# Gated attention kernel, one core: the first group's row step moved into the last feed-forward chunk, comparisons in two pieces, statistics on other half-steps

## The reference

```
xn = layernorm(x)                      # x: 8 batches x 1024 tokens x 512
q, k, v = xn @ Wq.T, xn @ Wk.T, xn @ Wv.T            # 16 heads of 32
attn = softmax(q @ k.T * 512 ** -0.5) + rel_bias     # the bias is added after the softmax
s = layernorm(attn @ v) * gamma + beta
h = square(relu(xn @ W_fc.T)); y = h @ W_proj.T      # W_fc: 2048 x 512
g = silu(spikes(y) / 5)                # spikes: how often a 5-step recurrence fires; 5 thresholds on y
out = x + s * g
```

## Time and profile before

| what | value |
|---|---|
| time, median of 3 runs (lowest to highest) | 3539.49 us (3537.76 to 3540.11) |
| the profiled execution: its time, its span | 3539.38 us, 3537.6 us |
| PE, ACT, DVE, POOL busy, share of the span | 97%, 74%, 71%, 49% |
| granted PE clock, mean | 0.996 of full speed (2.4 GHz) |
| feed-forward ends, attention begins | at about 1399 us of the span |

### The profile page before, as it was taken

How to read it: one execution, slowest core, us unless ns; L and a number is a source line. 1 busy time by engine, 2 the same in 40 slices (tenths; PEclk the granted TensorE clock), 3 DMA queues, 4 the chain that set the end, 5 groups by cost and what they waited for, 6 DMA issues and landing times.

```text
span 3537.6 us, 55268 instructions
## 1 busy us (share of the span) xinstructions
PE 3424.5 (97%) x19964; PEld 1440.8 (41%) x19964; DVE 2496.7 (71%) x3948; ACT 2628.4 (74%) x3926; POOL 1718.1 (49%) x997
## 2 busy tenths in 40 slices
PE   7999999999999999999999999999999999999996
PEld 3444444444444444433433433433433433433431
DVE  5555555555555545777888888888888788888887
ACT  6433333333333335999999999999999999999997
POOL 0012222111111123799675675675675675676662
PEclk9999999999999999999999999999999999999999
DMA  5122322332222222221422322322322322322322
GB/s 186 57 80 80 104 79 87 101 98 94 79 79 80 80 82 75 87 74 51 141 85 80 100 86 80 101 85 80 100 86 80 101 85 81 100 85 81 100 63 81
DMA packets 238751, 312.35 MB, mean 88 GB/s; under 512 B 96624, under 2 KB 132208, under 8 KB 238480
## 3 DMA queue, kind: packets, MB, share of 16 engines
q1 hardware_dynamic: 238480, 308.82, 28.1%
HBM read 174.65 MB, written 76.61 MB: 71 GB/s over the span
## 4 chain that ended last, share of the span: by engine, by line
ACT 37%; issue 10%; PE 8%; DVE 4%; SPq 1%; DMA 1%; ACTq 0%; DVEq 0%; POOL 0%; POOLq 0%
ACT recurrence_or_probs L1380 19%; ACT s_sb L1387 18%; DVE s_sb L1462 2%; PE misc L1249 2%; PE acc L1329 2%; PE s_ps L1309 2%; PE s_ps L1295 2%; DVE gate_or_tokens L1574 1%; DVE x_or_queries L1499 1%; SPq L253 0%; DMA xT<-xnT 0%; DVE outT L1482 0%; DVE gate_or_tokens L1577 0%; DMA x_or_queries<-sub_rows 0%; PE misc L1231 0%
## 5 line engine op out<-in xcount | busy, mean ns | idle before, releaser
L1462 DVE TENSOR_SCALAR_CACHE_REDUCE s_sb<-s_ps 128x1024 f32<-128x1024 f32 x998 | 1213.3, 1221 | 366.8 <-PE s_ps L1295 337.8
L1650 POOL TENSOR_TENSOR recurrence_or_probs<-recurrence_or_probs,toep 128x512 f32<-128x512 f32 (+1 forms) x375 | 1287.4, 3452 | 361.2 <-ACT recurrence_or_probs L1380 360.9
L1387 ACT ACTIVATE s_sb<-s_sb,nmax 128x1024 f32<-128x1024 f32 x998 | 1164.9, 1167 | 5.3 <-DVE s_sb L1462 5.3
L1380 ACT ACTIVATE recurrence_or_probs<-s_ps 128x1024 f32<-128x1024 f32 x1024 | 1059.3, 1036 | 6.5 <-PE s_ps L1309 6.4
L486 PE MATMUL ps_fc<-xnT_part,w_fc 128*128 128x512 f16 x3072 | 707.2, 380 | 4.5 <-DVE w_fc L734 4.5
L501 PE MATMUL ps_y<-w_pr,hid_part 128*128 128x512 f16 x3072 | 706.2, 380 | 3.5 <-issue 2.6
L127 POOL TENSOR_TENSOR recurrence_or_probs<-gate_or_tokens,beta_row 128x512 f32<-128x512 f32 x60 | 89.9, 1498 | 1110.0 <-DVE gate_or_tokens L182 1106.5
L658 ACT ACTIVATE relu<-ps_fc 128x512 f32<-128x512 f32 x256 | 152.8, 597 | 630.3 <-PE ps_fc L486 630.1
L842 DVE TENSOR_TENSOR hid<-relu 128x512 f32<-128x512 f32 x256 | 212.8, 831 | 510.4 <-ACT relu L658 510.4
L1329 PE MATMUL acc<-recurrence_or_probs,val 128*32 128x512 f32 x4096 | 545.1, 604 | 2.3 <-DVE recurrence_or_probs L1561 1.5
L486 PEld LDWEIGHTS ps_fc<-xnT_part,w_fc 128*128 128x128 f16 x3072 | 301.0, 98 | 368.9 <-issue 7.8
(11 more groups left out here) (172 smaller groups left out, 2673.1 us busy)
## 6 DMA issues: line engine op xcount, KB each, us to landing
toep<-table_rows SPq DMA_DIRECT2D x32, 2048.0 KB, 8.2
x_or_queries<-x_or_queries SPq DMA_DIRECT2D x384, 64.0 KB, 2.0
x_or_queries<-in_x SPq DMA_DIRECT2D x16, 1024.0 KB, 10.4
xnT<-xnT_part SPq DMA_DIRECT2D x32, 512.0 KB, 8.3
x_or_gate<-in_x SPq DMA_DIRECT2D x16, 1024.0 KB, 9.2
base<-x_or_gate SPq DMA_DIRECT2D x16, 1024.0 KB, 6.8
xT<-xnT SPq DMA_DIRECT2D x32, 512.0 KB, 9.6
result<-gate_or_tokens SPq DMA_DIRECT2D x64, 256.0 KB, 2.0
```

Source lines behind the costliest of these rows:

```text
L1380: nc.scalar.activation(prob[:, k % PROBS, 2 * second:2 * second + 2, :].rearrange("p j n -> p (j n)"), s_ps[:, item_buffer(pair_item(m)), ...
L1387: nc.scalar.activation(s_sb[:, i % 4, :], s_sb[:, i % 4, :], ACT.Exp, bias=nmax[:, par, j, st:st + 1], scale=-1.0, accum_out=den[:, par, j ...
L1462: nc.vector.tensor_scalar(s_sb[:, i % 4, :], s_ps[:, item_buffer(tile_item(n)), :], -1.0, None, ALU.mult, ALU.min, accum_out=nmax[:, par, ...
L1650: nc.gpsimd.tensor_tensor(tile, tile, toep[:, par, :, at:at + width], ALU.add).then_inc(biased, 1)
```

## The change

It has four parts, and the program computes the same values.

1. The row step of group 0 (logarithm, six POOL instructions, four matmuls, copy, four transfers) leaves the prelude and is placed in the last feed-forward chunk: the logarithm in step 10, the POOL instructions ahead of the gate's products, the matmuls in step 15 into `ps_t`, the copy in step 15, the transfers at the end of SP's chunk. The constants that it needs are written by POOL at the start of the program (`set_constants`) and no longer by DVE and POOL in the attention part.
2. In the last chunk the five counting instructions and the gate's are split into tile 0 (128x512) and tiles 1 to 3 (128x1536), with the second `first_max` of the step between the two.
3. The four `BN_STATS` of a slot move from half-steps 0, 1, 2, 3 to 0, 3, 5, 7, with what stands behind the last of them.
4. ACT's `root` of these slots moves from k = 4 to k = 6.

```diff
+    def set_constants(self, pool):
+        self.nc.gpsimd.memset(self.unit[:], 1.0).then_inc(self.sub_set, 1)
+        self.nc.gpsimd.memset(self.subT[:], 0.0).then_inc(self.sub_set, 1)
+        pool.wait_ge(self.sub_set, 2)
...
+    def load_rows(self, sp, qst, G, half):
+        sp.wait_ge(self.rows_read, G * 2 + half + 1)
+        for j in range(HG):
+            sp.dma_start(qst[ROWS:ROWS + SUBTRACTED, j, half * 512:(half + 1) * 512],
+                         self.sub_rows[j * HD:j * HD + SUBTRACTED, half, :]).then_inc(self.rows_loaded[half], 16)
...
+                if c == NC - 1:
+                    first.load_rows(sp, first.qst, 0, 0)
...
                     pool.wait_ge(first.ones_set, 1)
+                    first.subtracted(pool, 0, 0, 0)
...
+            def first_rows():
+                pe.wait_ge(first.max_done, FIRST_TILES)
+                first.rows(pe, ps_t[:, 0, :], w["identh"], 0, 0)
...
+                    if c == NC - 1 and f == FB - 1:
+                        first_rows()
                     if f >= LAG:
                         proj(c, f - LAG)
...
                         first_sum(2 * f - 5)
+                        if 2 * f - 5 == 15:
+                            first.ln_sums(act, 0, 0, 0)
...
+                    if c == NC - 1:
+                        if counting:
+                            spiking.count_spikes(c - 1, f - gate_at(c), slice(0, 1))
+                        if gating:
+                            spiking.gate_chunk(c - 1, slice(0, 1))
+                        if 0 <= 2 * f - 4 < FIRST_TILES:
+                            first_max(2 * f - 3)
+                        if counting:
+                            spiking.count_spikes(c - 1, f - gate_at(c), slice(1, 4))
+                        if gating:
+                            spiking.gate_chunk(c - 1, slice(1, 4))
+                        if f == FB - 1:
+                            first_rows_read()
...
-STATISTICS = {0: 0, 1: 1, 2: 2, 3: 3}
+STATISTICS = {0: 0, 3: 1, 5: 2, 7: 3}
...
-                if h == s.rows_0 and s.scores:
+                if h == ROWS_0 and s.scores and s.main:
                     rows(s.g + 1, 0)
...
-                    if k == 4 and s.finish and s.step == 0:
+                    if k == 6 and s.finish and s.step == 0:
                         root(s.done)
```

More of the change, by code:

```diff
@@ L245, in of_tile, with subtracted @@
         return i % 16 // 4, i // 16 * 4 + i % 4
+    def set_constants(self, pool):
+        self.nc.gpsimd.memset(self.unit[:], 1.0).then_inc(self.sub_set, 1)
+        self.nc.gpsimd.memset(self.subT[:], 0.0).then_inc(self.sub_set, 1)
+        pool.wait_ge(self.sub_set, 2)
+    def subtracted(self, pool, G, par, half):
+        n, sub, step = G * 2 + half, self.sub, self.sub_step
+        base = n * 6
+        pool.wait_ge(self.ln_done, n + 1)
+        wait(pool, self.rows_ps, n - 1)
+        wait(pool, step, base)
+        columns = lambda r: self.subT[:, half, :, :, r].rearrange("p q j -> p j q")
+        self.nc.gpsimd.tensor_tensor(sub[:, 0], self.nmax[:, par, :, half * 4:half * 4 + 4], self.lnd[:, half],
+                                     ALU.subtract).then_inc(step, 1)
+        for r in range(2):
+            pool.wait_ge(step, base + 2 * r + 1)
+            self.nc.gpsimd.tensor_tensor(columns(r), sub[:, r], self.unit[:], ALU.mult).then_inc(step, 1)
+            pool.wait_ge(step, base + 2 * r + 2)
+            self.nc.gpsimd.tensor_tensor(sub[:, r + 1], sub[:, r], columns(r), ALU.subtract).then_inc(step, 1)
+        pool.wait_ge(step, base + 5)
+        self.nc.gpsimd.tensor_tensor(columns(2), sub[:, 2], self.unit[:], ALU.mult).then_inc(step, 1)
@@ new lines, in ln_sums, with rows @@
+    def ln_sums(self, act, G, par, half):
+        act.wait_ge(self.sum_done, G * 32 + half * 16 + 16)
+        self.nc.scalar.activation(self.lnd[:, half], self.den[:, par, :, half * 4:half * 4 + 4], ACT.Ln).then_inc(self.ln_done, 1)
+    def rows(self, pe, bank, identh, G, half):
+        pe.wait_ge(self.sub_step, (G * 2 + half) * 6 + 6)
+        for q in range(4):
+            last = self.nc.tensor.matmul(bank[:, q * P:(q + 1) * P], self.subT[:, half, q].rearrange("p j r -> p (j r)"),
+                                         identh[:], start=True, stop=True)
+        last.then_inc(self.rows_ps, 1)
@@ L432, in _ @@
             pool.wait_ge(ident_step, 3)
+            first.set_constants(pool)
             for c in range(1, NC):
@@ L1191, in slot @@
                         store_tile(s.done, t)
-                if s.scores:
-                    load_rows(g + 1, op, 0)
+                if s.scores and s.main:
+                    first.load_rows(sp, qst[op], g + 1, 0)
                 if g == 3:
@@ L1268, in rows @@
                 take_misc()
-                pe.wait_ge(consts, CONSTS)
-                pe.wait_ge(sub_step, (G * 2 + half) * 6 + 6)
-                for q in range(4):
-                    last = nc.tensor.matmul(misc[:, q * P:(q + 1) * P], subT[:, half, q].rearrange("p j r -> p (j r)"),
-                                            identh[:], start=True, stop=True)
-                last.then_inc(rows_ps, 1)
+                first.rows(pe, misc, identh, G, half)
                 last_use[0] = (rows_read, G * 2 + half + 1)
@@ L1502, in take_qk @@
                                                ALU.mult, ALU.subtract).then_inc(qk_read, 1)
-            def take_rows(G, half):
-                dve.wait_ge(rows_ps, G * 2 + half + 1)
-                wait(dve, rows_loaded[half], G * 64)
-                nc.vector.tensor_copy(sub_rows[:, half, :], misc[:]).then_inc(rows_read, 1)
             def take_out(b, hg, half):
@@ L1588, in take_misc @@
                 if h == ROWS_1 and s.main:
-                    take_rows(s.g, 1)
+                    first.take_rows(dve, misc[:], s.g, 1)
                 if h in QUERY_KEYS and QUERY_KEYS[h][1] and s.project:
                     take_qk(s.g, QUERY_KEYS[h][0])
-                if h == s.rows_0 and s.scores:
-                    take_rows(s.g + 1, 0)
+                if h == ROWS_0 and s.scores and s.main:
+                    first.take_rows(dve, misc[:], s.g + 1, 0)
                 if h == s.out_0 and s.main:
```

116 lines of the change are left out of this document (50 added, 66 removed).

## The result

The changed kernel takes 3579.70 us (median of 4 runs, 3578.55 to 3584.17), the kernel before in the same series 3539.8 us. The ratio is 1.0115, with a 95% interval from 1.0098 to 1.0133: 1.15% slower.

The account below looks back on a forecast made before the run. PE was taken to bound up to 1420 us, ACT from 1420 to 3480 us. The sum: 3539.4 - 2.7 + 0.2 + 0.2 - 3.1 + 38.2 = 3572.2 us, given as 3572; range 3562 to 3580 us.

Parts of the forecast that it names:

- the hold: Half-step 7: POOL's bias, started 0.17 us earlier, holds the small `TENSOR_SCALAR`; ACT loses 2.73 us in 14 slots, 38.2 us.
- a dearer hold: Rival in the 14 slots: price up to 3.3 us each, 3580 us; chance 0.14 for a price off either way.
- The rival in which the statistics cost nothing: In the 14 slots the `TENSOR_SCALAR` gets in ahead of POOL's bias, ACT waits nothing: 3534.0 us; chance 0.15.
- Behind it nothing catches up, as ACT has no gaps to give back; the next maxima are in time again: After the held maximum in each slot: the 2.73 us stay lost, and no further loss is added.
- A second wait in the slot: Rival: `outT` late at half-step 6, so `weigh` and ACT wait 0.5 us in each slot: 3579 us; chance 0.04.
- The counting: Last chunk, steps 4 to 7: PE's wait for the maximum goes when the count is split, -2.7 us.
- The 0.6 us: Last chunk: assumed time of the count's first piece, between 0.57 and 0.69 us, before the maximum starts.
- lower bound of 2.3 us: Counting's gain if the first piece takes 0.69 us: some 0.1 us comes back in each of four steps.
- The row step: Moved into the last chunk: +0.2 us for four turning matmuls on PE's path, +0.2 us for POOL's instructions.
- The 0.2 us for POOL's six instructions: Last chunk, step 10: allowance for their overlap with DVE's squares, between nothing and about 0.6 us.
- The prelude: Without rows in `misc`, the second pair starts at 1417.77 instead of 1420.88: 3.1 us less.
- the wait that the prediction named: Prelude: the copy of the last keys takes over as the wait, losing 0.7 us of the first pair's gain.

Follow-up runs that it names:

- Experiments 3 and 4: Changed kernel with two (3) or one (4) more unread 128x16 POOL instructions ahead of the bias in the 14 slots: 3532.81 us and 3583.26 us.
- Experiment 7: Changed kernel with 20 more unread 128x256 matmuls on PE behind `weigh` of half-step 9 in the 14 slots: 3570.53 us.
- experiment 5: Changed kernel with the small instruction at half-step 7 as a TENSOR_TENSOR, epsilon from a 128x4 tile: 3580.55 us.
- experiment 12: Part 2 alone (counting and gate in two pieces) in the kernel before: 3538.95 us, ratio 0.9995.

## Why the prediction was right in the hold, wrong behind it, and 7.7 us low

The forecast was 3572 us and the median is 3579.70 us. That is the very edge of the range of 3562 to 3580 us, and as a ratio it lies past it: 3580 us is 1.0114 of the kernel before, 1.0115 were measured. The upper end of that range stood for a dearer hold, 3.3 us a slot; the hold cost 2.72 us, and the rest came by a way that the sum did not have. That the median still lies at the edge is luck.

**The hold: right.** The `TENSOR_SCALAR` was forecast at 4.4 us in 14 slots, 0.17 us behind the bias; it took 4.37 us and was 0.19 us behind. The price was forecast at 2.73 us and was 2.72 us. Experiments 3 and 4 show that the order of the two starts decides, and between them lie 0.2 us on POOL and 50 us of the whole. The rival in which the statistics cost nothing was rightly put at "0.17 us, and then in all 14 slots or in none"; it is what experiment 3 makes happen.

**"Behind it nothing catches up, as ACT has no gaps to give back; the next maxima are in time again": wrong.** This is the step that failed. It followed ACT alone behind the hold and put the term at zero. PE waits for the same maximum, which the prediction never asked; its clock falls to the 1.2 GHz level behind it, and ACT waits for PE's late pairs. The term measured 12.2 us in the profiled execution. Experiment 7 takes PE's wait away and leaves the hold: it gives back 9.2 us of the medians. With the measured term put in, the forecast of 3572 us becomes 3584 us for that execution (3584.17). The medians lie 39.9 us apart, and -5.5 + 38.1 us leave 7.3 us of it for this term in place of 12.2. The term differs from trace to trace: in experiment 5's, with falls in 11 slots and none of them of 6.8 us, it is 7.7 us. Whether the other three executions of the changed kernel had fewer or shorter falls is open. They have no traces, and their mean granted clocks, 0.990, 0.989 and 0.992 against the profiled one's 0.990, speak for it in the last alone. What lies ahead of step 2 of the last chunk scatters as well, by 3.4 us among the profiled executions (1298.1 to 1301.5 us, experiment 12).

**"A second wait in the slot", the rival at 3579 us: right in its time by luck, not in its mechanism.** It looked for the second wait at half-step 6 ahead of the hold, through `outT`. The second wait is behind the hold, through the clock.

**The counting: forecast -2.7 us, measured -2.3 us.** The 0.6 us were right: the maximum starts 0.60 us behind the start of the first piece (1313.38 to 1313.98), though the piece itself lasts 0.68 us. What is missing is in step 5, which takes 6.73 us instead of 6.37. PE waits there for 0.50 us ahead of the tile at 1325.41, for a maximum that DVE began late itself:

```profile
1323.45 0.19 ACT L706 ACTIVATION_READ_ACCUMULATOR xnT_part<-xnT_part,nmax 128x1 f32 x1
...
1324.12 1.22 DVE L916 TENSOR_SCALAR_CACHE_REDUCE xnT_part<-ps_t 128x1024 f32<-128x1024 f32 x1 [0.87 <-ACT xnT_part L706]
```

No piece of the count held this maximum: DVE had been idle for 0.87 us. It waited for ACT's exponential, which ended at 1323.64, and what held it for the other 0.48 us is open. So it is luck that the sum meets the prediction's lower bound of 2.3 us, which was worked out for a longer first piece.

**The row step: +0.4 us forecast, +0.2 us measured.** From step 2's `fc` to the first queries it is 101.80 us in the changed kernel and 101.60 us with part 2 alone. The 0.2 us for POOL's six instructions were not needed.

**The prelude: -3.1 us forecast, -3.09 us measured.** The first pair now starts at 1412.49, ahead of the copy of the last keys (1413.32), and PE's next use of `misc` waits for that copy: the wait that the prediction named.

## What to carry to other kernels

Ask of a moved instruction on DVE not how long it is but whether its form contends with GpSimd, and what GpSimd has just started; with 4 elements and one half-step's shift, 1.3% of the time hung on 0.2 us. In one program the order of the two starts held in all 14 slots, down to 0.01 us, but 0.2 us of other work on POOL turned it in all of them. So two tenths are no margin against the next edit: move the instruction by a whole step, or give it a form that is not held. And when a wait is priced, follow every engine that waits for the same buffer, PE above all, since a wait there can cost once more behind its end.

## What the runs showed of the hardware

- A `TENSOR_SCALAR` of 0.17 us that started 0.03 us behind a GpSimd `tensor_tensor` of 4.5 us lasted 4.53 us; ahead by 0.14 us it lasted 0.21 us and GpSimd's two biases took 9.07 instead of 9.03 us.
- `TENSOR_SCALAR` and `TENSOR_TENSOR`, SBUF to SBUF, were held (4.37 and 4.35 us). The accumulator form of `TENSOR_SCALAR` (0.16 us) and `BN_STATS` (0.69 us) were not.
- PE's granted clock fell to 0.50 behind a wait of some 2.58 us in 11 or 12 of 14 slots, behind 2.74 us in 13, behind 1.37 us in 6, behind 0.30 us in none. It fell 0.3 to 2.4 us behind the end of the wait, when PE was at work again.
- At 0.50, `weigh` (8 matmuls of 128x512, f32) took 1.94 us instead of 1.07.
- 280 matmuls whose result nobody reads made the kernel 9.2 us faster.
